# A top-128 attention on Trainium2: one masking step of the selection goes from VectorE to GpSimd

## The reference, cut to what matters

```python
draft = jnp.einsum('bhqd,bhkd->bhqk', qr, kr) + causal        # no scaling, keys of the future at -max
_, draft_indices = jax.lax.top_k(draft, 128)
mask = full(neg).at[..., draft_indices].set(0.0)              # and neg above the diagonal
attn = softmax(einsum('bhqd,bhkd->bhqk', qr, kr) / sqrt(32) + mask)
out = einsum('bhqk,bhkd->bhqd', attn, v)
```

## Time and profile before

| what | value |
|---|---|
| median of 3 runs | 6185.69 us (6176.85 to 6195.40) |
| the profiled execution: span, first to last instruction | 6177.2 us |
| VectorE busy | 3892.3 us, 63% of the span |
| ScalarE busy | 3356.3 us, 54% |
| TensorE busy | 4809.9 us, 78% |
| GpSimd busy | 263.0 us, 4% |

### The profile page before, as it was taken

The page is one execution under the profiler, slowest core; times in us unless marked ns, Lnnn a source line. Parts: engine busy times, 40 slices in busy tenths (PEclk is TensorE's granted clock), DMA queues, the critical chain, the costliest instruction groups (busy, mean ns, idle before and its releaser), DMA issues. The chain is left out here.

```text
span 6177.2 us, 81244 instructions
## 1 busy us (share of the span) xinstructions
PE 4809.9 (78%) x23480; PEld 3476.0 (56%) x23480; DVE 3892.3 (63%) x11322; ACT 3356.3 (54%) x7666; POOL 263.0 (4%) x149
## 2 busy tenths in 40 slices
PE   7997999999999989944667667767666666766787
PEld 2446888888744444423546546645645655656444
DVE  2654555555522335638888888888888888885222
ACT  1213555454400002148888888888888888884001
POOL 1330000000000003300000000000000000000000
PEclk9998999999999999975555555555555555555888
DMA  2223111112121122320110000110010010000211
GB/s 113 70 65 78 46 44 44 44 44 47 44 95 44 48 81 64 71 49 8 22 22 22 18 22 5 22 22 22 18 22 12 15 22 22 22 1 5 86 61 54
DMA packets 275861, 249.37 MB, mean 40 GB/s; under 512 B 170240, under 2 KB 210320, under 8 KB 275472
## 3 DMA queue, kind: packets, MB, share of 16 engines
q1 hardware_dynamic: 274928, 245.08, 15.0%
q0 software_dynamic: 544, 0.07, 0.0%
HBM read 167.51 MB, written 77.59 MB: 40 GB/s over the span
## 5 line engine op out<-in xcount | busy, mean ns | idle before, releaser
L894 ACT ACTIVATE a_sign<-a_x,a_state 128x256 bf16<-128x256 f32 (+6 forms) x2240 | 1832.4, 819 | 311.1 <-DVE a_state L1015 196.9
L839 PE MATMUL a_ps_o<-a_v,a_probT 128*128 128x32 f32 x4608 | 1018.0, 389 | 343.6 <-ACT a_probT L870 342.6
L839 PEld LDWEIGHTS a_ps_o<-a_v,a_probT 128*128 128x128 f32 x4608 | 1037.4, 333 | 368.0 <-ACT a_probT L870 367.5
L820 PE MATMUL a_ps_s<-a_k,a_q 128*128 128x512 bf16 (+3 forms) x1536 | 493.2, 464 | 592.7 <-DVE a_x L1122 552.3
L831 PE MATMUL a_ps_t<-a_ident,a_prob 128*128 128x128 f32 x2304 | 601.8, 425 | 151.0 <-DVE a_prob L1112 147.4
L629 ACT ACTIVATE a_prob<-a_ps_s,a_shift 128x128 f32<-128x128 f32 (+7 forms) x512 | 379.7, 742 | 561.6 <-DVE a_shift L657 447.6
L321 PE MATMUL p_ps_qkv<-p_w,p_hT 128*128 128x512 f32 x1536 | 675.5, 597 | 3.3 <-ACT p_hT L359 2.3
L820 PEld LDWEIGHTS a_ps_s<-a_k,a_q 128*128 128x128 bf16 x1536 | 162.7, 129 | 831.0 <-DVE a_x L1122 660.5
L831 PEld LDWEIGHTS a_ps_t<-a_ident,a_prob 128*128 128x128 f32 x2304 | 509.7, 254 | 161.0 <-issue 138.3
L607 PE MATMUL a_ps_o<-a_v,a_probT 128*128 128x32 f32 x4608 | 594.0, 276 | 0.0
L607 PEld LDWEIGHTS a_ps_o<-a_v,a_probT 128*128 128x128 f32 x4608 | 566.4, 195 | 27.1 <-issue 4.5
(11 more groups left out here) (177 smaller groups left out, 5582.0 us busy)
## 6 DMA issues: line engine op xcount, KB each, us to landing
a_q<-qk SPq DMA_DIRECT2D x256, 256.0 KB, 4.7
qk<-p_qkT SPq DMA_DIRECT2D x32, 960.0 KB, 6.2
p_h<-h SPq DMA_DIRECT2D x32, 512.0 KB, 7.0
a_k<-qk SPq DMA_DIRECT2D x256, 64.0 KB, 5.0
o<-a_o SPq DMA_DIRECT2D x32, 512.0 KB, 3.3
m_o<-o SPq DMA_DIRECT2D x32, 512.0 KB, 5.3
m_h<-h SPq DMA_DIRECT2D x32, 512.0 KB, 4.9
p_w<-in_wqkv SPq DMA_DIRECT2D x16, 768.0 KB, 11.5
```

The source lines that it names most:

```text
L820: nc.tensor.matmul(ps_s[:, n % 2, a:a + w], q[:, y, head, i * P:(i + 1) * P], k[:, y, a:a + w], start=(y == 0), stop=False, skip_group_che ...
L839: mm = nc.tensor.matmul(ps_o[:, n, :], probT[:, n % 2, b * P:(b + 1) * P], v[:, b * DH:(b + 1) * DH], start=(b == 0), stop=(b == i))
L894: ins = nc.scalar.activation(sign[:, off(i):off(i) + w], x[:, par, at:at + w], ACT.Sign, scale=-1.0, bias=state[:, par, 0, n:n + 1], accum ...
```

## The change

GpSimd gets a program in this stage. For each ranked tile, in the order `RANK_ORDER`, it waits until VectorE's count has written `above` and until the eight largest of the tile two back have been taken from `below`, then makes `below` in two instructions: `above * -1e30 + 0`, and the sum of that with the scores. VectorE no longer has the masking instruction. It counts tile c and then takes the eight largest of tile c-2, for which it waits on GpSimd; it has no drain between them. `above` gets a third buffer. The tiles of the parts stay as they were, but the eight largest now run two tiles behind across the parts, and part 2 ends with those of the last three tiles.

```diff
--- before.py
+++ after.py
@@ -717,7 +717,7 @@
         probT = sb("probT", [P, 2, T])
         o = sb("o", [P, TT, G * DH])
         sign = sb("sign", [P, SEG], BF16)
-        above = sb("above", [P, 2, T], BF16)
+        above = sb("above", [P, 3, T], BF16)
         below = sb("below", [P, 2, T])
         top, shift = sb("top", [P, 2, 2 * TT]), sb("shift", [P, 2, 2 * TT])
         total, inv = sb("total", [P, 2, 2 * TT]), sb("inv", [P, 2 * TT])
@@ -743,6 +743,7 @@
         s_done, x_ready = sem("s_done"), sem("x_ready")
         t_ready, signs_done = sem("t_ready"), sem("signs_done")
         exp_done, prob_ready = sem("exp_done"), sem("prob_ready")
+        above_ready, below_ready, nine_ready = sem("above_ready"), sem("below_ready"), sem("nine_ready")
         turn_done, probT_ready, pv_done, o_ready = sem("turn_done"), sem("probT_ready"), sem("pv_done"), sem("o_ready")
 
         def ps_seg(m, i):
@@ -754,6 +755,7 @@
 
         ALL = dict(score=True, search=True, keep=True, value=True)
         FIRST_LOOP, LOOPS = 4, (PAIRS - 6) // 2
+        RANK_ORDER = [*range(0, TT - 2), TT - 1, TT - 2, *range(TT + 1, NS), TT]
 
         def over_slots(eng, slot):
 
@@ -925,6 +927,30 @@
                                 exps(n, par)
 
                 over_slots(act, slot)
+
+            @block.gpsimd
+            def _(pool):
+                def slot(s, par, st):
+                    y = 1 - par
+
+                    def mask_above(c):
+
+                        n = RANK_ORDER[c]
+                        m, i = RANKED[n]
+                        at, w = ps_seg(m, i), (i + 1) * P
+                        out = below[:, c % 2, 0:w]
+                        wait_alone(pool, above_ready, (s - 1) * NS + (c + 1), const_in, 64)
+                        if not (isinstance(s, int) and s == 1 and c < 2):
+                            wait_alone(pool, nine_ready, (s - 1) * NS + (c - 1), const_in, 64)
+                        nc.gpsimd.tensor_scalar(out, above[:, c % 3, 0:w], MASKED, 0.0, ALU.mult, ALU.add)
+                        pool.drain()
+                        nc.gpsimd.tensor_tensor(out, out, x[:, y, at:at + w], ALU.add).then_inc(below_ready, 1)
+
+                    if st["keep"]:
+                        for c in range(NS):
+                            mask_above(c)
+
+                over_slots(pool, slot)
 
             @block.vector
             def _(dve):
@@ -1016,28 +1042,28 @@
                         if p < PASSES - 1:
                             ins.then_inc(t_ready, 1)
 
-                    def rank_steps(n, r):
-
-
+                    def count_above(c):
+
+                        n = RANK_ORDER[c]
                         m, i = RANKED[n]
                         at, w = ps_seg(m, i), (i + 1) * P
-                        tl = state[:, y, 0, n:n + 1]
-                        return (
-                            lambda: nc.vector.tensor_scalar(above[:, r, 0:w], x[:, y, at:at + w], tl, None, ALU.is_ge,
-                                                            ALU.add, accum_out=exact[:, n:n + 1]),
-                            lambda: nc.vector.scalar_tensor_tensor(out=below[:, r, 0:w], in0=above[:, r, 0:w],
-                                                                   scalar=MASKED, in1=x[:, y, at:at + w], op0=ALU.mult,
-                                                                   op1=ALU.add),
-                            lambda: nc.vector.max(nine[:, n, 1:9], below[:, r, 0:w]),
-                        )
-
-                    def rank_some(mine):
-                        todo = [rank_steps(n, k % 2) for k, n in enumerate(mine)]
-                        for c in range(len(mine) + 2 if todo else 0):
-                            for d in (2, 1, 0):
-                                if 0 <= c - d < len(mine):
-                                    todo[c - d][d]()
-                            dve.drain()
+                        nc.vector.tensor_scalar(above[:, c % 3, 0:w], x[:, y, at:at + w], state[:, y, 0, n:n + 1], None,
+                                                ALU.is_ge, ALU.add,
+                                                accum_out=exact[:, n:n + 1]).then_inc(above_ready, 1)
+
+                    def nine_below(c):
+
+                        n = RANK_ORDER[c]
+                        w = (RANKED[n][1] + 1) * P
+                        wait_alone(dve, below_ready, (s - 1) * NS + (c + 1), const_in, 64)
+                        nc.vector.max(nine[:, n, 1:9], below[:, c % 2, 0:w]).then_inc(nine_ready, 1)
+
+                    def rank_some(first, last):
+
+                        for c in range(first, last):
+                            count_above(c)
+                            if c >= 2:
+                                nine_below(c - 2)
 
                     def choose():
 
@@ -1158,14 +1184,17 @@
                         dve.nop()
                         dve.drain()
 
-                    RANKS = [[*range(0, TT - 2), TT - 1], [TT - 2, *range(TT + 1, NS)], [TT], (), ()]
+                    RANKS = [(0, TT - 1), (TT - 1, NS - 1), (NS - 1, NS), (0, 0), (0, 0)]
                     KEEPS = [(), (), range(0, 4), range(4, 14), range(14, 2 * TT)]
 
                     def part(p):
 
                         if st["keep"]:
-                            rank_some(RANKS[p])
+                            rank_some(*RANKS[p])
                             if p == 2:
+                                nine_below(NS - 2)
+                                nine_below(NS - 1)
+                                dve.drain()
                                 choose()
                                 exact_where_needed()
                         if p == 2 and st["value"]:
```

## The result

The changed kernel takes 6278.2 us (median), the kernel before 6181.3 us in the same comparison: ratio 1.0158, 95% interval 1.0139 to 1.0178, or +97 us. The forecast was +42. The direction held, the size is more than twice the forecast.

The account below looks back on a forecast made before the run. The bound changes within a slot: ScalarE in parts 0 and 1, VectorE in parts 2 to 4. 17 x 2.0 + 12 x (2.0 - 1.0) - 4.5, about +42 us, gave 6228 us (own range 6210 to 6250; 8 in 10: 6205 to 6300).

Parts of the forecast that it names:

- what bounds what: Within a slot, ScalarE's signs set parts 0 and 1 (42.2 us); VectorE's work sets parts 2 to 4 (48.4 us).
- The split by inputs: VectorE beside GpSimd: two-input instructions wait for GpSimd's work to end (1.75 us), one-input ones run as before (0.14 us).
- part 2: End of narrow(1) to `choose`: 2.08 us before, 2.05 us later after the change, taken as 2.0, with no cover.
- the 17 slots: Slots without a long stall at the loop's jump back: parts 0 and 1 stay at 42.2 us, each slot loses 2.0.
- the 12: Slots with a long stall behind the loop's jump back: each loses 2.0 less 1.0 us.
- the term of GpSimd's tile: GpSimd's masking of one tile costs 3.02 ns per column plus 0.28 us.
- The margin of 0.9 us: Part 1: GpSimd's masks end at 19.0 of about 19.9 us, ahead of narrow(1).
- Their -1.0: Parts 0 and 1 of slots behind the loop's jump fall from 43.45 to about 42.4 us as VectorE's masking goes.
- -4.5 for VectorE's freed time: Slot 1 and the slot behind the last search, where VectorE alone sets the ranking: -4.5 us for both together.
- The rival that I gave 0.14: GpSimd falls behind: above 1.16 ns per column its masking runs into narrow(1); some +235, 6421 us; chance 0.14.
- The stall ahead of L1140: Faster rival: VectorE's 3.45 us stall behind the branch over exact selection goes; 6128 us if in all slots; chance 0.03.
- the last rival's +550: VectorE doesn't get free: one-input counts and eight largest in parts 0 and 1 held too; +550, 6780 us; chance 0.01.

Follow-up runs that it names:

- e1: Kernel before, VectorE still masking, but eight largest taken two tiles behind its counts and across the parts, GpSimd idle: 6228.2 us, ratio 1.0078.
- e2: Kernel before, with the one tile ranked in part 2 ranked at the end of part 1 instead: 6158.0 us, ratio 0.9972.
- e3: Changed kernel, with GpSimd's product written as bf16 over the marks, so its sum has one bf16 input: 6242.5 us, ratio 1.0107.
- e7: Changed kernel, all 14 tiles ranked in parts 0 and 1, VectorE masking five and GpSimd nine, product still f32: 6104.9 us, ratio 0.9879.
- e5: Changed kernel, plus eight GpSimd sums of 256 columns behind its last masking in each slot, which nothing waits for: 6341.2 us, ratio 1.0261.

## Why the prediction was wrong

*Right: what bounds what.* Parts 0 and 1 go at ScalarE's pace, and VectorE's freed time turned into idle time there; parts 2 to 4 are paid one for one (e1, e2). Counts and eight-largest are no slower beside GpSimd: 867 and 826 ns on average in the changed kernel, 875 and 828 in the earlier trace rows. The split by inputs, which the prediction took from the earlier trace rows, doesn't hold for every instruction: the narrowing's one-input comparison (L1022) is held too.

*Nearly right: part 2.* Forecast +2.05, measured 4.32 - 2.08 = +2.24, with the idle stretch ahead of the last eight-largest where I put it. Parts 2 to 4 grew by more in the 17 slots (2.67) and less in the 12 (1.85); the records put the rest on short waits for nothing shown, ahead of fetches above all, which change place from program to program. What sets them stays open.

*Wrong: the term of GpSimd's tile.* I took 3.02 ns per column and 0.28 us for the gaps: 2.21 us at the mean width of 640. The traces give 0.725 (product) + 1.545 (sum) + 0.23 (gaps) = 2.50. The sum is 0.24 of that miss, because I scaled one row of 1280 columns to zero, which hides the 0.19 us that every sum costs at any width, and because that row's second input is bf16 (e3); the product's hidden 0.19 us makes 0.10. Seven tiles: part 0's masks end 18.2 us after the threshold in slot 15, forecast 16.3, and 0.4 us into narrow(0); part 1's end at 20.5 after narrow(0), forecast 19.0, behind the signs. The margin of 0.9 us that I had written down was smaller than the error of the price it rested on.

*What followed.* The 17 slots lost 0.3 us in parts 0 and 1 in place of nothing. In the 12 I had seen the overlap at narrow(0) and missed that the one at narrow(1) follows: the signs of pass 1 catch up with the delay, GpSimd does not. Their -1.0 is there in e1 and turned to +1.4. At the ends I had -4.5 for VectorE's freed time. Slot 1 instead waits for GpSimd in both narrowings, so its parts 0 and 1 grow by 0.8, and its parts 2 to 4 grow by 4.0: 2.0 as in e1, and about as much in a wait of 2.23 us ahead of a fetch for nothing shown. The end of the stage grows by 3.1, of which 2.0 stand in slot 31, whose part 2 I had taken to be off the path. Against the forecast's sum: 17 x (2.99 - 2.0) + 12 x (3.26 - 1.0) + (4.8 + 3.1 + 4.5) = 16.8 + 27.1 + 12.4, some 56 of the 57 us between the forecast's 41.5 and the span's 98.8. Some 34 of them stand in parts 0 and 1 of the 29 slots, and so go back to the price of the tile; e3's cheaper sum wins 28 of these back.

*The rival that I gave 0.14*, GpSimd falling behind, is what happened in kind: its masks run past the signs of pass 1 into narrow(1), the first sign of being wrong that the prediction names. Its price was too high for where it began (0.9 us of margin became 0.5 of overlap), and it came in by the sum and the fixed parts, not by the product's rate, on which alone I had hung it: that is 0.83 ns, under the 1.16 that I had set as the point of change. The stall ahead of L1140 stayed (89.1 us in the changed kernel). One sum was wrong and changed nothing: the last rival's +550 already holds part 2's 2.0 us, so it gives about 6736 us and not 6780.

The Trainium skill (GPSIMD Engine Reference, "Engine selection") put two-input work at about half VectorE's speed, and from a time on the same page I had estimated 2.2 ns per column, but let the row decide. The traces agree: 1.545 us at 640 columns against the 0.811 us of VectorE's masking, 1.9 times, and 2.36 us for 1024 columns, 2.3 ns each with the fixed part. The page was nearer than my row.

## What to carry to other kernels

Before work goes to another engine, ask of each stretch which engine sets it: here the freed time lay where ScalarE did, and the added latency where VectorE did. Price an engine's instruction from rows of two widths with the same input types; one row scaled to zero hides the fixed part, and a margin must be larger than that error. Where two engines hold each other, let the helper end ahead of the many small instructions that come next, and split the tiles between the engines until it does.

## What the runs showed of the hardware

The hold goes both ways. In e7 a VectorE masking, two inputs, starts just ahead of a GpSimd sum of 768 columns:

```profile
4041.16 1.09 DVE L1073 SCALAR_TENSOR_TENSOR a_below<-a_above,a_x 128x896 f32<-128x896 bf16 x1
```

```profile
4041.20 2.74 POOL L958 TENSOR_TENSOR a_below<-a_below,a_x 128x768 f32<-128x768 f32 x1
```

The sum takes 2.74 us where its group's mean is 1.81 in the changed kernel: 0.93 longer. In slot 14 of e7 the same two met in the other order, and the masking was the one that waited, 2.44 us in place of 1.09:

```profile
3955.33 2.44 DVE L1073 SCALAR_TENSOR_TENSOR a_below<-a_above,a_x 128x896 f32<-128x896 bf16 x1 [0.46 <-issue]
```

```profile
3955.00 1.82 POOL L958 TENSOR_TENSOR a_below<-a_below,a_x 128x768 f32<-128x768 f32 x1
```

Two kinds of VectorE instruction with a single input were held as well. One is the comparison of 14 columns (L1022): in the changed kernel it met a sum in 12 slots between 3000 and 5400 us. In 8 of them the sum had started 0.23 us earlier, and the comparison took 0.55 us; in 4 the comparison started 0.05 us ahead of the sum and took its usual 0.18. The other is the CAST of 32 columns in e5, 0.58 us against 0.18. Counts, eight-largest and the reductions in e5 were not held. The rows don't show what makes the difference. The Trainium skill (SBUF — State Buffer, "Who interferes with whom") states that the shared ports are an exclusive lock for whoever issues first, and that a cast can take them in a faster mode. The traces agree with both, in the numbers above, though no run here isolates the cast.
